# Ones filled ahead of chunk 1's rows, a bias spread by ScalarE, and routing behind the statistics, in an attention and expert kernel

## The reference, cut to what matters

```python
xn = (x - mean) / sqrt(var + 1e-5)                  # x: 16 x 256 rows of 128
# attention, 16 heads of 8, 64 random features a head, inside each batch of 256 rows
q, k, v = xn@Wq + bq, xn@Wk + bk, xn@Wv + bv
qp, kp  = relu(q @ rw) + 1e-6, relu(k @ rw) + 1e-6
out     = (qp @ (kp.T @ v)) / (qp @ kp.sum(rows) + 1e-6)
attn    = out @ Wo + bo
# one of 8 experts a row, chosen by the router, gated by its share of the top two
logits  = xn @ wr + br
ffn     = (gelu(xn@w1[e] + b1[e]) @ w2[e] + b2[e]) * gate
result  = x + attn + ffn
```

## Time and profile before

| | |
|---|---|
| median of 3 runs | 203.91 us (203.34 to 204.15) |
| the profiled execution | 203.84 us |
| its span in the trace | 202.1 us |
| TensorE matmul busy | 188.3 us, 93% of the span |
| VectorE, ScalarE, GpSimd busy | 135.8, 132.7, 123.4 us |
| granted TensorE clock, mean | 0.989 |

### The profile page before, as it was taken

One profiled execution on the slowest core, in us unless ns is written; L12 is line 12 of the kernel. 1 busy time (PEld: TensorE's weight loads), 2 busy tenths in 40 slices (PEclk: granted clock), 3 DMA queues, 4 the chain that ended last, 5 costly groups with the idle time before them and its releaser, 6 DMA issues.

```text
span 202.1 us, 6867 instructions
## 1 busy us (share of the span) xinstructions
PE 188.3 (93%) x2329; PEld 150.5 (74%) x2329; DVE 135.8 (67%) x468; ACT 132.7 (66%) x319; POOL 123.4 (61%) x157
## 2 busy tenths in 40 slices
PE   6899896999999999999999989999999999999970
PEld 6566564666666666666666768999999999999960
DVE  5869799477889777777777886455455455455440
ACT  3287756879877777777777764756656656656630
POOL 2156795111157766666665220688888888888885
PEclk9999999999999999999999999999999999999995
DMA  4820699999812212222229392598999999997231
GB/s 131 247 85 14 158 211 181 112 306 291 222 56 67 82 65 65 68 71 64 72 66 287 96 261 82 143 262 174 208 208 202 223 203 211 213 212 149 27 28 11
DMA packets 32609, 29.49 MB, mean 146 GB/s; under 512 B 6048, under 2 KB 24896, under 8 KB 32576
## 3 DMA queue, kind: packets, MB, share of 16 engines
q1 hardware_dynamic: 25792, 24.82, 48.1%
q0 software_dynamic: 6784, 4.24, 15.6%
HBM read 20.10 MB, written 11.56 MB: 157 GB/s over the span
## 4 chain that ended last, share of the span: by engine, by line
PE 71%; DVE 11%; ACT 5%; POOL 4%; DMA 3%; issue 3%; SPq 2%; DVEq 0%; POOLq 0%; ACTq 0%
PE feat L693 16%; PE o_bank L705 8%; PE feat L572 8%; PE feat L705 8%; PE feat L554 7%; PE o_bank L613 7%; PE kv_bank L587 6%; PE o_bank L625 3%; PE kv_bank L597 2%; POOL out L456 2%; DVE bv_mat L979 2%; DMA bk_col<-in_bk 2%; DVE stats L889 2%; DMA out<-k_all,slots_all 2%; POOL rows_all L390 1%
## 5 line engine op out<-in xcount | busy, mean ns | idle before, releaser
L456 POOL DMA_INDIRECT out<-k_all,slots_all x39 | 60.9, 1561 | 21.9 <-DMA out<-res 10.0
L857 ACT ACTIVATE q_all<-feat,w_slot 128x128 f32<-128x128 f32 x156 | 44.5, 369 | 30.3 <-PE feat L693 30.3
L693 PE MATMUL feat<-v_all,w_slot 128*128 128x128 f32 x312 | 41.2, 275 | 0.8 <-ACT v_all L862 0.8
L426 POOL DMA_INDIRECT sorted_x<-rows_all,place_i x32 | 31.5, 986 | 15.7 <-PE feat L572 8.8
L693 PEld LDWEIGHTS feat<-v_all,w_slot 128*128 128x128 f32 x312 | 38.0, 192 | 1.1 <-issue 1.1
L421 POOL TENSOR_SCALAR o_bias<-kv_sum,den_eps 128x1 f32<-128x1 f32 x32 | 9.2, 286 | 25.5 <-DVE kv_T L1076 19.5
L705 PE MATMUL o_bank<-w_sb,q_all 128*128 x160 | 21.2, 276 | 0.2 <-issue 0.2
L390 POOL TENSOR_SCALAR rows_all<-x_all,meanvar,rstd 128x128 f32<-128x128 f32 x16 | 13.2, 833 | 12.2 <-DVE rstd L901 12.2
L1133 DVE SCALAR_TENSOR_TENSOR gated_b<-b_all,slots_all,out_row 128x128 f32<-128x128 f32 x39 | 13.7, 352 | 10.1 <-issue 10.1
L705 PE MATMUL feat<-w_sb,q_all 128*128 x152 | 20.1, 275 | 0.0
L800 ACT ACTIVATE k_feat<-feat 128x512 f32<-128x512 f32 x16 | 9.6, 597 | 15.7 <-PE feat L554 15.7
(11 more groups left out here) (151 smaller groups left out, 321.4 us busy)
## 6 DMA issues: line engine op xcount, KB each, us to landing
w_slot<-w1x SPq DMA_DIRECT2D x39, 258.0 KB, 3.9
sorted_x<-ones_f SPq DMA_DIRECT2D x1, 2535.0 KB, 21.1
w1x<-in_w SPq DMA_DIRECT2D x1, 2048.0 KB, 26.4
out<-res SPq DMA_DIRECT2D x16, 128.0 KB, 2.8
x_all<-in_x SPq DMA_DIRECT2D x7, 256.0 KB, 4.0
slots_all<-sorted_x SPq DMA_DIRECT2D x23, 65.0 KB, 3.8
out<-k_all,slots_all POOLq DMA_INDIRECT x39, 4.9
slots_all<-sorted_x SPq DMA_DIRECT2D x1, 520.0 KB, 4.8
```

Source lines behind the costliest of these rows:

```text
L426: pool.indirect_dma_start(sorted_x, bass.IndirectOffsetOnAxis(ap=place_i[:, t:t + 1], axis=0), rows_all[:, t, :], None).then_inc(x_moved, 16)
L456: pool.indirect_dma_start(out_rows, bass.IndirectOffsetOnAxis(ap=slot_rows[j % SLOT_RING][:, D + 1:XW].bitcast(I32), axis=0), y_sb[j % Y_R ...
L693: ins = pe.matmul(bank[:, a * P:(a + 1) * P], w1_slot[j % W1_RING][:, a * P:(a + 1) * P], xsT[j % X_RING][:, :], start=True, stop=True)
L857: act.activation(hidden_T[j % H_RING][:, a * P:(a + 1) * P], hid_bank[j % HID][:, a * P:(a + 1) * P], ACT.Gelu, bias=w1_slot[j % W1_RING][ ...
```

## The change

GpSimd fills the ones in three groups (batches 0 to 5, 6 to 11, 12 to 15): after VectorE's six mask steps, after VectorE has normalised chunk 0, and behind its own tile of chunk 1. It takes one tile of chunk 2 where it took two, and makes `ones_b` and `rank_w` later. The waits for `mask_ready` 8 go from the head of the attention stage to `key_values(0)` on TensorE and to the third iteration on VectorE. VectorE runs all chunks' statistics first, with half of the next chunk's statistics ahead of each `row_scale`; the routing of chunks 0 and 1 stands ahead of the last `row_scale`, and the rest between the saves of v. ScalarE makes `bv_mat`, takes the roots of chunks 5 to 7 earlier, and waits for less. `wts_in` is split in three. The empty put stands behind the last `r_ready`, and its wait behind all the puts.

```diff
-NORM = [0, 1, 2, 2, 2] + [3] * (CHUNKS - 5)
+NORM = [0, 1, 1, 2, 2, 2] + [3] * (CHUNKS - 6)
+ONES = [0, 6, 12, NBATCH]
+MASK_STEPS = 6
@@ sync: Wq, Wk on wqk_in; x of chunk 1; then
-            sp.dma_start(wvr_sb[:, 0:D], Wv).then_inc(wts_in, 16)
-            sp.dma_start(wvr_sb[:, D:VW], wr).then_inc(wts_in, 16)
-            sp.dma_start(bq_col...).then_inc(wts_in, 16)
-            sp.dma_start(bk_col...).then_inc(wts_in, 16)
+            sp.dma_start(bq_col...).then_inc(bqk_in, 16)
+            sp.dma_start(bk_col...).then_inc(bqk_in, 16)
+            sp.dma_start(wvr_sb[:, 0:D], Wv).then_inc(wvr_in, 16)
+            sp.dma_start(wvr_sb[:, D:VW], wr).then_inc(wvr_in, 16)
@@ gpsimd
-            pool.memset(ones_b[:, :], 1.0).then_inc(consts_ready, 1)
             pool.iota(row_i[:, :], [[0, 1]], base=0, channel_multiplier=1).then_inc(mask_ready, 1)
+            pool.wait_ge(route, MASK_STEPS)
+            ones_of_v(ONES[0], ONES[1])
+            pool.wait_ge(xn_dve, 1)
+            ones_of_v(ONES[1], ONES[2])
+            normalise(1)
+            ones_of_v(ONES[2], ONES[3]).then_inc(mask_ready, 1)
             then(pool.iota(rank_i[:, :, :], [[0, RT], [-1, E]], base=E, channel_multiplier=0))
             pool.tensor_copy(rank_w[:, :, :], rank_i[:, :, :]).then_inc(rank_ready, 1)
-            for c in range(1, 4):
+            for c in range(2, 4):
                 normalise(c)
...
-            for b in range(NBATCH):
-                ins = pool.memset(strided(v_all[:, K * b, DK:DK + 1], [(VS, K), (2 * DK, H), (1, DK)]), 1.0)
-            ins.then_inc(mask_ready, 1)
+            pool.memset(ones_b[:, :], 1.0)
...
+            pool.wait_ge(r_ready, NBATCH)
             pool.indirect_dma_start(out_rows, ...).then_inc(primed, 16)
-            pool.wait_ge(primed, 16)
             for u in range(R_RING):
                 pool.wait_ge(r_stored[u], 16 * NBATCH // R_RING)
             for j in range(SLOTS):
                 put(j)
+            pool.wait_ge(primed, 16)
@@ tensor: consts_ready 2 becomes 1; first projection
-            pe.wait_ge(wts_in, 16 * 6)
+            pe.wait_ge(wqk_in, 16 * 2)
@@ scalar
-            act.wait_ge(wts_in, 16 * 6)
+            act.wait_ge(bqk_in, 16 * 2)
             for c in range(CHUNKS):
                 if c < EARLY:
                     save_qk(c, 0)
-                if c == 1:
-                    deviation(3)
+                if c in (1, 3):
+                    deviation(3 if c == 1 else 6)
                 if c + 1 < CHUNKS:
                     save_xnT(c + 1)
-                if c == 0:
-                    deviation(2)
+                if c in (0, 2, 4):
+                    deviation({0: 2, 2: 5, 4: 7}[c])
...
+                if c == EARLY:
+                    act.wait_ge(bias_in, 16 * (2 + H))
+                    act.activation(bv_mat[:, :], ident[:, :], ACT.Identity, scale=0.0, bias=bv_col[:, 0:1]).then_inc(bv_ready, 1)
@@ vector
-            for c in range(4):
-                row_stats(c)
+            for c in range(CHUNKS):
+                row_stats(c, 1 if c >= 3 else 0)
+                if 2 <= c < CHUNKS - 1:
+                    half_stats(c + 1, 0)
+                if c == CHUNKS - 1:
+                    find_top(0)
+                    pick(0)
                 row_scale(c)
                 normalise(c)
-            row_stats(4)
-            for c in range(LATE):
...
+            for c in range(V_DVE, LATE):
+                save_v(c)
                 if c == V_DVE:
                     dve.wait_ge(bias_in, 16 * (2 + H))
                     dve.tensor_scalar(den_eps[:, :], ...).then_inc(bits_ready, 1)
-                    dve.tensor_copy(bv_mat[:, :], strided(bv_col[:, 0:1], [(0, P)])).then_inc(bv_ready, 1)
+                if c < LATE - 1:
+                    find_top(c - V_DVE + 1)
+                    pick(c - V_DVE + 1)
```

More of the change, by code:

```diff
@@ L202, in build @@
         x_half = sem("x_half")
-        wts_in, wo_in, rw_in = sem("wts_in"), sem("wo_in"), sem("rw_in")
+        wqk_in, bqk_in, wvr_in = sem("wqk_in"), sem("bqk_in"), sem("wvr_in")
+        wo_in, rw_in = sem("wo_in"), sem("rw_in")
         br_in, bias_in, b2_in = sem("br_in"), sem("bias_in"), sem("b2_in")
@@ L293, in _ @@
             sp.dma_start(x_all[:, 1, :], x_b[1]).then_inc(x_in[0], 16)
-            sp.dma_start(wq_sb[:, :], Wq).then_inc(wts_in, 16)
-            sp.dma_start(wk_sb[:, :], Wk).then_inc(wts_in, 16)
+            sp.dma_start(wq_sb[:, :], Wq).then_inc(wqk_in, 16)
+            sp.dma_start(wk_sb[:, :], Wk).then_inc(wqk_in, 16)
             load_x(1)
-            sp.dma_start(wvr_sb[:, 0:D], Wv).then_inc(wts_in, 16)
-            sp.dma_start(wvr_sb[:, D:VW], wr).then_inc(wts_in, 16)
-            sp.dma_start(bq_col[:, :], bq.rearrange("(p a) -> p a", a=1)).then_inc(wts_in, 16)
-            sp.dma_start(bk_col[:, :], bk.rearrange("(p a) -> p a", a=1)).then_inc(wts_in, 16)
+            sp.dma_start(bq_col[:, :], bq.rearrange("(p a) -> p a", a=1)).then_inc(bqk_in, 16)
+            sp.dma_start(bk_col[:, :], bk.rearrange("(p a) -> p a", a=1)).then_inc(bqk_in, 16)
+            sp.dma_start(wvr_sb[:, 0:D], Wv).then_inc(wvr_in, 16)
+            sp.dma_start(wvr_sb[:, D:VW], wr).then_inc(wvr_in, 16)
             load_x(2)
@@ L383, in _, with ones_of_v @@
                                pattern=[[-1, P]], channel_multiplier=1).then_inc(consts_ready, 1)
-            pool.memset(ones_b[:, :], 1.0).then_inc(consts_ready, 1)
             pool.iota(row_i[:, :], [[0, 1]], base=0, channel_multiplier=1).then_inc(mask_ready, 1)
+            def ones_of_v(first, last):
+                for b in range(first, last):
+                    ins = pool.memset(strided(v_all[:, K * b, DK:DK + 1], [(VS, K), (2 * DK, H), (1, DK)]), 1.0)
+                return ins
             def normalise(c):
@@ L490, in project_v @@
                 s = c % 2
+                if c == 0:
+                    pe.wait_ge(wvr_in, 16 * 2)
                 for h in range(CB):
@@ L501, in keep_warm @@
                     pe.transpose(xnT_bank[1][:, (t % CT) * P:(t % CT + 1) * P], ident[:, :], ident[:, :])
-            pe.wait_ge(consts_ready, 2)
+            pe.wait_ge(consts_ready, 1)
             keep_warm(20)
@@ L579, in key_values @@
                 v_in(pe, b + 1 if b > 0 else CB * CHUNKS)
+                if b == 0:
+                    pe.wait_ge(mask_ready, 8)
                 pe.wait_ge(k_act, 2 * b + 2)
@@ L637, in _ @@
             pe.wait_ge(qk_saved, 2 * LATE)
-            pe.wait_ge(mask_ready, 8)
             for i in range(NBATCH):
@@ L775, in _ @@
                     save_qk(c, 0)
-                if c == 1:
-                    deviation(3)
+                if c in (1, 3):
+                    deviation(3 if c == 1 else 6)
                 if c + 1 < CHUNKS:
                     save_xnT(c + 1)
-                if c == 0:
-                    deviation(2)
+                if c in (0, 2, 4):
+                    deviation({0: 2, 2: 5, 4: 7}[c])
                 if EARLY <= c < LATE:
                     save_qk(c, 0)
-                if 1 < c < CHUNKS - 3:
-                    deviation(c + 3)
                 if c < LATE:
@@ L829, in save_turned @@
                 act.activation(ka[i % 2][:, :], (kv_ps_t if i < NBATCH else kt_bank)[:, 0:S], ACT.Copy).then_inc(ka_ready, 1)
-            act.wait_ge(mask_ready, 8)
             for i in range(NBATCH):
@@ L947, in _, with row_stats @@
             then(dve.tensor_scalar(den_one[:, :], bit_f[:, 1:2], EPS, None, ALU.mult))
-            def row_stats(c):
-                for h in range(CB):
+            def row_stats(c, first=0):
+                for h in range(first, CB):
                     half_stats(c, h)
@@ L1079, in mask_kv @@
                                              accum_out=kv_sum[s][:, par:par + 1]).then_inc(kv_ready, 1)
-            dve.wait_ge(mask_ready, 8)
             k_relu(0)
@@ L1088, in _ @@
                 if i == 2:
+                    dve.wait_ge(mask_ready, 8)
                     scan_rows()
```

## The result

The twelve executions of the changed kernel have a median of 204.03 us and lie between 200.09 and 205.66; before has 204.89 in its twelve (203.34 to 206.59). By these medians the change is worth 0.9 us, where 4.1 was forecast, and 204.03 is outside the range of the prediction. The ratio to before is 0.9866 (95% interval 0.9817 to 0.9914), about 2.7 us less, but it leaves out as slow every execution more than 1.5% above the fastest of its kernel, so that three of the changed kernel's twelve are left in it (200.09, 202.75 and 202.83 us). The profiled execution took 204.42 us (span 202.4) and is not among the three. The lowest, 200.09, is 0.4 above the forecast; it has no trace.

A forecast was written before the change was run, and what follows sets the result against it. The front was held by waits, not by TensorE; the later stretch would only shift. Gains 0.46 + 1.88 + 1.98 − 0.2 = 4.12 us off 203.84 gave 199.72, with the median 0.07 above the profiled execution: forecast 199.7 us, range 199.0 to 201.6.

The forecast's parts named there:

- Part 1: Start of the front: split weight waits and earlier mask steps and statistics bring the first projection to 7.51, gaining 0.46 us.
- Part 2: Front, q projections: the new order has the rows ready in time, so three excesses totalling 1.88 us go.
- Part 3: Stall at 27.5 us: without copy and memsets there, v saves come in time and 1.98 us go.
- Part 4: What comes late next, at the first features: ScalarE's table load is no longer hidden, costing 0.2 us.
- My last rival: Long copy slow for another reason, or attention waits on an unmoved transfer (sorted rows' fill): 202.7 us, chance 0.04.
- one of my own signs of being wrong: Before 50 us: the granted clock falling below 1.00 would show the forecast wrong; no size given.
- Part 5: Front: the 16 memsets in three groups beside VectorE's work cost nothing; bounds nothing to 4.1 us.
- one of its rivals: Chunk 1: VectorE's third tile waits 1.03 us behind the last four memsets, 0.7 counts: 200.4 us, chance 0.07.
- Part 6: End of attention: the empty put, released at 123.84, takes about 1.57 us, leaves 1.9 us and costs nothing.
- The sum: Whole kernel: 0.46 + 1.88 + 1.98 − 0.2 = 4.12 us gained, forecast 199.7 us.

The follow-up runs named there:

- e4: Changed kernel with 30 more identity turns on TensorE ahead of the first projection; 217.81 us against 219.07 before, ratio 0.9950.
- e19: Changed kernel with VectorE's and ScalarE's old order and old tile split, w1 and w2 issued behind b1; 217.17 us against 218.76 before, ratio 0.9920.
- e20: Changed kernel with the whole w1 and w2 transfers issued later, behind b1; 215.76 us against 218.76 before, ratio 0.9852.
- e12: Changed kernel with bv_mat's copy back on VectorE, behind the save of chunk 4; one execution, 217.44 us against 218.84 before.
- e5: Changed kernel unaltered, run a second time; 216.60 us against 218.85 before, ratio 0.9917.
- e1: Changed kernel unaltered; 217.50 us against 219.07 before, ratio 0.9917.
- e6: Changed kernel with w1 and w2 in eight pieces each behind the stores of attention results; 216.24 us against 218.85 before, ratio 0.9882.
- e7: Changed kernel with the last four memsets of ones waiting until VectorE has normalised chunk 1; 216.97 us against 218.85 before, ratio 0.9872.
- e8: Changed kernel with w1 and w2 in eight pieces and the last four memsets behind VectorE's chunk 1 tiles; 215.74 us against 218.85 before, ratio 0.9846.
- e17: Changed kernel with w1 and w2 issued behind b1 and the last four memsets behind VectorE's chunk 1 tiles; 214.94 us against 218.76 before, ratio 0.9816.
- e18: Kernel before with w1 and w2 issued behind b1; 218.99 us against 218.76 before, ratio 1.0006.
- e11: Kernel before with only bv_mat moved to ScalarE, memsets left in place; one execution, 219.38 us against 218.84 before.
- e2: Changed kernel with w1 and w2 in eight pieces each behind the stores of attention results; 216.67 us against 219.07 before, ratio 0.9899.

## Why the prediction was wrong, by its own steps

**Part 1** held in kind: 0.26 us, not 0.46, in the pair of traces above. Statistics start at 3.02, 0.04 earlier, not 0.13; the first projection follows ScalarE at 7.71. Even the 0.26 is not clear of the spread: over the other traces the first projection starts at 7.53 to 8.23 with the new front (e4 aside) and at 7.73 to 7.80 with the old one.

**Part 2** held from chunk 1 on. The q projections of chunks 1 to 3 are 3.1 us apart, that of chunk 4 comes 3.5 behind, where the order changes, and the next two 3.1; no matmul waits for GpSimd's tiles (two loads do, 0.3 and 0.2 us), and chunk 7's turn is not late. The order was worth 1.9 us at the features (e19 against e20, from the first q projection on), which is the 1.88 that I had put on it, and 1.4 us in time.

**Part 3** held: no save is late, the constants are done by 28 us. That it does not need `bv_mat` on ScalarE, e12 shows. From the first q projection to the features the kernel before takes 25.62 us and e19 24.46, the third tile's 0.72 included, so 25.62 − 24.46 + 0.72 = 1.88 us are left for the memsets and `bv_mat` together, where I had 1.98.

**Part 4** was the step that failed. ScalarE's table load costs about 0.1 us (k's relu at 31.54, the features done at 31.41), where I had 0.2. But "what comes late next" is TensorE's own code. I had no term for it, that is, had put it at nothing, and had argued from 68.00 busy of 69.00 us that the stage behind the front could only shift. That row begins at 50 us. In the stretch ahead of it the DMA engines were full in the kernel before, share 1.14, and I drew nothing from it:

```profile
33.50:50.00 16.50, 16.04 (x236) 10.46 (x240) 11.69 (x48) 12.96 (x22) 2.07 (x6) 1.00 1.14 221
```

My last rival, a transfer whose landing does not move with the front, was of the right kind, with a chance of 0.04 and the wrong transfer: the fill, for which GpSimd waits, and not the code block, for which nothing waits by name. The price was 1.2 us in e5, 2.9 in e1, and all of 3.6 us with the lower clock in the profile shown first. There one of my own signs of being wrong came true as well: the clock fell below 1.00 before 50 us. Whether the other executions of that comparison near 204 us had the same gap and clock, no trace shows.

**Part 5** was wrong by one of its rivals. The third tile of chunk 1 waited for the four last memsets, and features started 0.72 us later for it: from the first q projection on they come at 22.55 us in e1, e5, e6 and e20, and at 21.83 or 21.84 in e7, e8 and e17. For this I had a chance of 0.07 and a price of 0.7. I had taken as evidence against it that the tiles ran beside a GpSimd tile; that is another instruction than a memset. Statistics beside memsets cost nothing, as taken: 0.86 to 0.90 for four.

**Part 6** held. The empty put:

```profile
124.67 1.64 POOL L473 DMA_INDIRECT out<-ones_f  x1 [8.55 <-DVE res L1061]
127.31 1.57 POOL L467 DMA_INDIRECT out<-k_all,slots_all  x1 [1.00 <-DMA out<-res]
```

It ends 1 us before the stores release the first put.

**The sum** of 4.1 us is close to what the change can give: e17, with both obstacles out of the way, starts the features 4.0 us and iteration 3 4.4 us earlier than the kernel before with the same transfers (e18), and ends 3.8 us earlier than before. Parts 2 and 3 are the sound ones: without the third tile's wait they gave 3.8 us (25.62 − 21.84) of the 3.86 that I had put on them; part 1 gave 0.3 or less of its 0.46. As changed, 1.6 and 2.3 us of it reached the end in e1 and e5; in the first comparison it was 0.9 by the medians and 2.7 by the ratio.

## What to carry to other kernels

When a front is made shorter, ask of every transfer in flight behind it whether its landing moves too, and count the engine's own code among them: a gap named "issue" in the middle of a group without waits, at the same instruction in every execution, was here a block of code that had not come. Large loads that are needed late may be better issued behind the crossing that they would delay than as early as possible; here this gave 3.0 to 4.0 us under before in place of 1.6 to 2.3. Keep back-to-back memsets on GpSimd away from any VectorE copy or tensor_scalar between SBUF and SBUF: one of two columns stood for 4.63 us here.

## What the runs showed of the hardware that was not expected

- A VectorE copy or tensor_scalar between SBUF and SBUF that met a row of GpSimd memsets did not get in between two of them: it stood for the whole row, 4.63 us beside sixteen (e11), 1.0 us longer beside four. In e11 it had started before the first of them (27.23 against 27.58), while GpSimd's last tile still ran. The Trainium skill, SBUF — State Buffer, section "Who interferes with whom", has a VectorE instruction in a two-port mode and GpSimd shut one another out, whoever issues first holding the shared ports for its instruction. The rows agree that one is shut out; what they add is that the row of memsets acted as one.
- After a gap of 2.19 us the granted clock fell, and groups of 1.00 and 1.08 us took 1.72 and 1.73. After gaps of 2.47 us in e1 and 2.19 in e7 it stayed at 1.00. What decides was not found, and only this one trace shows the fall.
- TensorE went on 1.4 to 1.6 us after the late packet had landed, in each of the seven traces with a gap.
- The same kernels took 7% longer in all later comparisons, on three chips, at a granted clock of 1.00: between 60 and 110 us the features of keys took 16.4 us for 127 matmuls in e1 and 11.5 for 160 in the first trace of the changed kernel, other groups the same as there. This was not explained, nor was why the spread pieces cost the iterations 1 us in e2.
